# Second mixture: its first eight tiles from what two of four groups of rows fill, with the table of tiles made in two halves

## What is computed

```python
ln1_out = _layernorm(hidden_states, ln1_weight, ln1_bias)
...                                   # attention over pairs, projection
hidden_after_attn = hidden_states + proj_out
ln2_out = _layernorm(hidden_after_attn, ln2_weight, ln2_bias)
x = ln2_out.reshape(-1, H)            # H = 256
gate = jax.nn.softmax(jnp.einsum('th,eh->te', x, router_weight), axis=-1)
top_probs, top_idx = jax.lax.top_k(gate, TOP_K)           # TOP_K = 2 of 8 experts
h_mid = jax.nn.gelu(jnp.einsum('th,ehf->etf', x, moe_w1)) # 256 -> 512
expert_out = jnp.einsum('etf,efh->eth', h_mid, moe_w2)    # 512 -> 256
weights = jnp.sum(jnp.where(top_idx[None] == e_ids, top_probs[None], 0.0), axis=-1)
moe_out = jnp.einsum('eth,et->th', expert_out, weights).reshape(S, B, H)
return hidden_after_attn + moe_out
```

## Time and profile before

| | |
|---|---|
| median of 3 runs | 1021.64 us (1018.97 to 1023.74) |
| profiled execution | 1022.95 us, span of its instructions 1021.2 us |
| TensorE busy with products | 906.8 us (89%) |
| VectorE busy | 801.2 us (78%) |
| ScalarE busy | 731.2 us (72%) |
| POOL busy | 605.9 us (59%) |
| mean granted clock of TensorE | 0.938 |

### The profile page before, as it was taken

The page is one execution under the profiler, slowest core; times in us unless marked ns, Lnnn a source line. Parts: engine busy times, 40 slices in busy tenths (PEclk is TensorE's granted clock), DMA queues, the critical chain, the costliest instruction groups (busy, mean ns, idle before and its releaser), DMA issues. The chain is left out here.

```text
span 1021.2 us, 22434 instructions
## 1 busy us (share of the span) xinstructions
PE 906.8 (89%) x6180; PEld 805.9 (79%) x6180; DVE 801.2 (78%) x2324; ACT 731.2 (72%) x1651; POOL 605.9 (59%) x699
## 2 busy tenths in 40 slices
PE   7899999999999999999999848879966751799997
PEld 5579989999999999998989736669945551599996
DVE  7589999999999999999989798757657786244443
ACT  2378889899899999999989747326654741566663
POOL 2298878877777676765555354660265278145444
PEclk8999999999999999999999968999978875799999
DMA  9276666777666666676666140347762624254453
GB/s 309 55 204 192 191 181 189 194 198 201 184 196 189 191 190 189 191 213 168 212 178 194 46 154 16 117 151 227 240 207 63 238 91 153 75 81 74 76 84 48
DMA packets 111427, 162.14 MB, mean 159 GB/s; under 512 B 16201, under 2 KB 85193, under 8 KB 110282
## 3 DMA queue, kind: packets, MB, share of 16 engines
q1 hardware_dynamic: 100200, 140.56, 46.3%
q0 software_dynamic: 10224, 18.00, 8.3%
q10 hardware_dynamic: 882, 2.14, 0.7%
HBM read 110.31 MB, written 25.17 MB: 133 GB/s over the span
## 5 line engine op out<-in xcount | busy, mean ns | idle before, releaser
L2380 POOL TENSOR_SCALAR probs<-probs,inv_sum 128x1024 f32<-128x1024 f32 (+3 forms) x128 | 303.2, 2368 | 6.7 <-DVE inv_sum L2547 6.7
L2526 DVE TENSOR_TENSOR pT_lo<-t_ps,pT_hi 128x512 fp32r<-128x512 f32 (+1 forms) x320 | 198.3, 634 | 9.1 <-ACT pT_hi L2410 7.0
L2438 ACT ACTIVATE probs<-probs,neg_max 128x1025 f32<-128x1025 f32 (+7 forms) x256 | 196.8, 771 | 5.3 <-DVE neg_max L2501 5.3
L2410 ACT ACTIVATE pT_hi<-t_ps 128x512 fp32r<-128x512 f32 (+1 forms) x320 | 172.7, 551 | 31.5 <-PE t_ps L2617 18.0
L2501 DVE CUSTOM_DVE_ANT_0 probs<-s_ps,bias_set,neg_null 128x512 f32<-128x512 f32 (+3 forms) x256 | 160.6, 645 | 2.2 <-PE s_ps L2582 2.0
L2617 PE MATMUL t_ps<-ident,probs 128*128 128x128 f32 x1152 | 157.6, 273 | 0.2 <-POOL probs L2380 0.2
L2617 PEld LDWEIGHTS t_ps<-ident,probs 128*128 128x128 f32 x1152 | 136.8, 141 | 24.1 <-issue 2.3
L2632 PE MATMUL o_ps<-pT_hi,values 128*128 128x256 f32 x576 | 148.4, 287 | 1.0 <-DVE pT_lo L2526 1.0
L2581 PE MATMUL s_ps<-k_hi,q_hilo 128*128 128x512 f32 (+3 forms) x384 | 144.7, 380 | 4.1 <-DVE q_lo L2517 1.5
L2633 PE MATMUL o_ps<-pT_lo,values 128*128 128x256 f32 x576 | 145.6, 281 | 0.0
L2582 PE MATMUL s_ps<-k_lo,q_one 128*128 128x512 f32 (+3 forms) x384 | 133.7, 348 | 0.0
(11 more groups left out here) (385 smaller groups left out, 2155.8 us busy)
## 6 DMA issues: line engine op xcount, KB each, us to landing
bias_set<-bias_dram SPq DMA_DIRECT2D x16, 1024.0 KB, 5.4
bias_set<-bias_dram SPq DMA_DIRECT2D x16, 896.0 KB, 5.3
bias_set<-bias_dram SPq DMA_DIRECT2D x16, 768.0 KB, 4.9
bias_set<-bias_dram SPq DMA_DIRECT2D x16, 640.0 KB, 4.5
q_hilo<-q_hi SPq DMA_DIRECT2D x128, 64.0 KB, 2.0
q_hilo<-q_lo SPq DMA_DIRECT2D x128, 64.0 KB, 2.0
q_one<-q_hi SPq DMA_DIRECT2D x128, 64.0 KB, 2.1
bias_set<-bias_dram SPq DMA_DIRECT2D x16, 512.0 KB, 5.5
```

The source lines that it names most:

```text
L2380: pool.tensor_scalar(keys, keys, inv_sum[:, x.set, 0, h:h + 1], None, ALU.mult).then_inc(normed, 1)
L2410: act.activation(pT_hi[n % 3][:, 0:count, :], t_ps[n % 3][:, 0:2 * P * count], ACT.Copy).then_inc(hi_out, 1)
L2438: act.activation(p, p, ACT.Exp, scale=-1.0, bias=neg_max[:, x.set, row.unit, h:h + 1], accum_out=row_sum[:, x.set, row.unit, h:h + 1]).the ...
L2526: dve.tensor_tensor(pT_lo[n % 3][:, 0:count, :], t_ps[n % 3][:, 0:2 * P * count].rearrange("p (n q) -> p n q", n=count), pT_hi[n % 3][:, 0 ...
```

## The change

Four things change.

The table is made by a new class, `SplitTable`. `first_half` runs on VectorE after `sum_up(1)`, from the slabs as groups 0 and 1 left them: it counts only full tiles (`full_tiles`), of which there are at least nine, and makes the first eight entries. The rest (`second_half`) is cut into four parts, which run on VectorE inside the second mixture, ahead of its first tiles' outputs; it places what is left of each expert behind the full tiles. The experts are therefore gone through twice: the sequence of tiles is now expert 1 (4 tiles), 2 (5), 5 (3), and then 1 (6), 2 (5), 3, 4 (3), 5 (5), 6, 7 (3), 36 in all.

SP loads the first eight tiles after the scatters of groups 0 and 1 (`early_scattered`) and the stores of groups 0 to 2 (`first_stored`), and stores group 3 and writes the padding behind these loads. The wait for padding, late scatters and the rest of the table moves ahead of tile 8.

On VectorE `weights_low(4)` moves from ahead of the gates of group 2 to behind `sum_up(3)`, `sum_up(2)` moves ahead of `place(2)`, and `make_table` between `place(3)` and the last three `weights_low` goes away.

On TensorE, POOL and VectorE the mixture's waits for words are cut in two in the same way. The wait for all weights stands behind the turning of the first two tiles.

```diff
+class SplitTable:
+    FULL = EARLY_GROUPS * GROUP * TOP
...
+    def first_half(self, dve, room, ready, words_ready, clear_ready):
+        these = slice(0, self.FULL)
+        now = slice(0, BUFS)
+        self.tiles(dve, rt.full_tiles, EARLY_GROUPS, -(P - 1) / (2.0 * P))
+        self.firsts(dve, rt.full_first, rt.full_tiles)
...
+        begun, over, tile_row = self.place(dve, room, these, rt.full_first, rt.full_end, rt.full_row)
...
+        dve.tensor_copy(rt.row_of[:, now], rt.rows_f[:, now]).then_inc(ready, 1)
...
+    def second_half(self, dve, part, ready, words_ready, clear_ready):
+        rest = slice(BUFS, ROUTED)
+        if part == 0:
+            self.tiles(dve, rt.n_tiles, GROUPS, (P - 1) / (2.0 * P))
+            self.settle(dve, dve.tensor_tensor(rt.n_tiles[:], rt.n_tiles[:], rt.full_tiles[:], ALU.subtract))
+            self.firsts(dve, rt.first_tile, rt.n_tiles)
...
@@ pair_attention_stage, sync @@
+            for g in range(GROUPS - 1):
+                store(g, first_stored)
+            sp.wait_ge(table_ready, 1)
+            at = first_rows(nc, rt, len(first))
+            sp.wait_ge(first_stored, 16 * (GROUPS - 1) * B)
+            sp.wait_ge(early_scattered, 16 * EARLY_GROUPS * GROUP * TOP)
+            for k in range(len(first)):
+                sp.dma_start(first[k], routed_rows[bass.ds(at[k], P), :]).then_inc(first_in[k], 16)
+            store(GROUPS - 1, last_stored)
             sp.wait_ge(slabs_ready, 1)
             store_padding(sp, nc, rt, routed_rows, padded)
-            sp.wait_ge(table_ready, 1)
-            at = first_rows(nc, rt, len(first))
-            sp.wait_ge(stored, 16 * (1 + GROUPS * B))
-            sp.wait_ge(padded, 16 * E)
-            sp.wait_ge(scattered, 16 * NT * TOP)
-            for k in range(len(first)):
-                sp.dma_start(first[k], routed_rows[bass.ds(at[k], P), :]).then_inc(first_in[k], 16)
@@ pair_attention_stage, vector @@
             sum_up(1)
+            table.first_half(dve, table_room, table_ready, words_ready, clear_ready)
             shifts(1, 3)
-            weights_low(4)
             gates(2)
             choose(2)
             top_weights(2)
+            sum_up(2)
             place(2)
-            sum_up(2)
             sum_up(3)
+            weights_low(4)
             gates(3)
             choose(3)
             top_weights(3)
             place(3)
-            make_table(dve, rt, table_step, table_ready, slabs_ready, words_ready)
+            table.slabs(dve, slabs_ready)
             weights_low(5)
             weights_low(6)
             weights_low(7)
@@ second_mixture_stage @@
         def _(sp):
+            sp.wait_ge(table_ready, 2)
+            sp.wait_ge(padded, 16 * E)
+            sp.wait_ge(scattered, 16 * (GROUPS - EARLY_GROUPS) * GROUP * TOP)
...
             for i in range(ROUTED):
                 low(i + 3)
                 hidden_low(i + 1)
+                if i < 3:
+                    table.second_half(dve, i + 1, table_ready, words_ready, clear_ready)
...
             turn_rows(0)
             turn_rows(1)
+            pe.wait_ge(words_ready, 1)
+            words = expert_words(nc, rt, mybir.EngineType.PE, 0, 1)
+            pe.wait_ge(w_lo_ready, E)
             up(0)
```

More of the change, by code:

```diff
@@ L1056, in pair_attention_stage @@
 def pair_attention_stage(nc, block, sbuf, psum, sem, aps, keep, routing, routed_rows, parts, out):
-    xs, yacc, ident, power4, w2, w2_hi, w_in, w_used, scattered, smalls, loaded, first, first_in, w_proj, done_sems, first_pair, words_ready, w_lo_ready, out_stored = keep
+    xs, yacc, ident, power4, w2, w2_hi, w_in, w_used, scattered, smalls, loaded, first, first_in, w_proj, done_sems, first_pair, words_ready, w_lo_ready, out_stored, table, early_scattered, second_sems = keep
     ln1_w, ln1_b, ln2_w, ln2_b, w_qkv, w_router = smalls
@@ L1088, in pair_attention_stage @@
         table_room = lT[1][0:1].rearrange("o c n -> o (c n)")
-        rt.begun, rt.over, rt.tile_row = (table_room[:, ROUTED * E * i:ROUTED * E * (i + 1)].rearrange("o (n e) -> o n e", e=E)
-                                          for i in range(3))
         gate = sbuf(st, "pa_gate", [P, GROUP, E])
@@ L1144, in _, with store @@
             sp.dma_start(out[T:OUT_ROWS, :].rearrange("(n p) d -> p n d", p=P),
-                         rt.padding[:, 0:D].unsqueeze(1).broadcast_to([P, 1 + SPARES, D])).then_inc(stored, 16)
+                         rt.padding[:, 0:D].unsqueeze(1).broadcast_to([P, 1 + SPARES, D])).then_inc(last_stored, 16)
             tiles = out[0:T, :].rearrange("(n p) d -> p n d", p=P)
-            for g in range(GROUPS):
+            def store(g, stored):
                 sp.wait_ge(summed, g + 1)
@@ L1937, in second_mixture_stage @@
 def second_mixture_stage(nc, block, sbuf, psum, sem, keep, ln, routing, routed_rows, target):
-    ident, w_hi, w_lo, rows, rows_in, y, words_ready, w_lo_ready = keep
+    ident, w_hi, w_lo, rows, rows_in, y, words_ready, w_lo_ready, scattered, table, second_sems = keep
     ln_w, ln_b, w_qkv = ln
@@ L2045, in hidden_low @@
                 dve.tensor_tensor(h_lo[i % 2][:], h_ps[i % 2][:], h_hi[i % 2][:].bitcast(F32), ALU.subtract).then_inc(h_lo_ready, 1)
-            dve.wait_ge(words_ready, 2)
-            of = experts(nc, rt, mybir.EngineType.DVE)
             low(0)
             low(1)
+            dve.wait_ge(words_ready, 1)
+            words = expert_words(nc, rt, mybir.EngineType.DVE, 0, 1)
+            table.second_half(dve, 0, table_ready, words_ready, clear_ready)
             low(2)
@@ L2081, in up @@
                     cols = slice(F2 * c, F2 * c + F2)
-                    high, low = (w[:, bass.ds(of(i), 1), cols] for w in (w_hi, w_lo))
+                    high, low = (w[:, bass.ds(expert_in(words, i), 1), cols] for w in (w_hi, w_lo))
                     pe.matmul(u_ps[i % 2][:], x_hi[i % 2][:, c, :], high, start=(c == 0), stop=False)
@@ L2115, in _ @@
                 turn_rows(i + 3)
+                if i + 2 == BUFS:
+                    pe.wait_ge(words_ready, 2)
+                    words = words + expert_words(nc, rt, mybir.EngineType.PE, 1, WORDS)
                 up(i + 2)
@@ L3092, in program @@
                     w2_hi = sbuf(second, "w2_hi", [P, E, W2COLS], F32R)
+                    rt.place_split(sbuf, second)
                     rows = [flat(xs)[:, ROW * i:ROW * i + ROW] for i in range(BUFS)]
@@ L3096, in program @@
                                                                    (ln1_w, ln1_b, ln2_w, ln2_b, w_qkv, w_router), loaded,
-                                         rows, rows_in, inputs.w_raw, done, first_pair, second_words, w2_lo_ready, out_stored), rt, routed_rows, parts, out)
+                                         rows, rows_in, inputs.w_raw, done, first_pair, second_words, w2_lo_ready, out_stored, table, early_scattered,
+                                         second_sems), rt, routed_rows, parts, out)
                     middle.close()
                     second_mixture_stage(nc, block, sbuf, psum, sem, (ident[:], w2_hi, w2, rows, rows_in, [yacc[:, i, :] for i in range(BUFS)],
-                                                                 second_words, w2_lo_ready),
+                                                                 second_words, w2_lo_ready, second_scattered, table, second_sems),
                                          (ln2_w, ln2_b, w_qkv), rt, routed_rows, out)
```

160 lines of the change are left out of this document (100 added, 60 removed).

## The result

The changed kernel takes 1004.14 us in the median of four runs (1002.52 to 1004.81), the kernel before 1022.69 beside it (four runs, 1018.97 to 1026.75). The ratio is 0.9828, with a 95% interval of 0.9802 to 0.9853: by the ratio 17.6 us less, by the two medians 18.6. The prediction was 1008.6, with a range of 1003.5 to 1017.

What follows compares the result with a forecast made beforehand. TensorE's 24.5 us hole, closed by a chain over POOL's scatters and SP's loads, was taken as the bound. 18.0 − 3.9 − 1.1 = 13.0 us gained, so median 1021.64 becomes 1008.6, range 1003.5 to 1017.

Steps and rivals of the forecast that it cites:

- The likeliest case: Whole kernel: TensorE's hole closes 18.0 us earlier, then late rows cost part of it; 1008.6 us, chance 0.62.
- the places of the rows: Second mixture: tile i+8 loads into tile i's place only after its accumulation, limiting the gain to 9.5 to 16.5 us.
- The 858.9: TensorE's first up-product: predicted start in us, low weights done at 858.2 plus 0.43 for the first low half, against 876.93.
- First half of the table: VectorE, from the sum of group 1: 25 instructions taking 4.3 us unpaused; could be 10 with pauses.
- pauses in the table: VectorE's first half: 5.0 us of old pauses recur, or SP stalls at two lists; gain 5 to 9.5 us, chance 0.20.
- SP's queue: SP, third store to tile 8: stalled entries at 0.75 us each put the end some 20 us late; chance 0.04.
- Placing of group 2, 0.65 us late: VectorE: a sum ahead of the placing starts it at about 842.3, not 841.65, delaying POOL's late scatters.
- first accumulation at 876.5: POOL: late scatters end at 873.1, then reading words takes at most 3.1 us; the old start was 887.55.
- So it waits 3.9 us in all over tiles 8 to 10: TensorE: tile 10's rows arrive at 892.4 but are wanted at 888.6, leaving 14.1 of the 18.0 us.
- My bound on the gain, 890.6 less the first accumulation: Whole kernel: gain is 890.6 minus POOL's first accumulation start, 9.5 to 16.5 us for starts between 881 and 874.
- Second half of the table and later words, 1.1 us: Second mixture: table pieces on VectorE and word reading on TensorE's queue cost 1.1 us; bounds 0 and 5.
- POOL is not held: POOL: weight instructions do not hold its scatters, so tile 10's rows come in time; 1004.5 us, chance 0.08.

Runs made afterwards that it cites:

- late_rows: The changed kernel, but SP loads the first eight tiles at the old place, behind the fourth store, padding and all scatters: 1023.63 us, ratio 0.9976.
- pool_delay6: The changed kernel with 20 chained memsets on POOL between its last scatter and the first accumulation: 1017.58 us, ratio 0.9933.
- scatter_late: The changed kernel with POOL held for 12 chained memsets ahead of its last four scatters: 1003.93 us in its one run.
- order_alone: The kernel before with only VectorE's new order, table and SP unchanged: 1025.03 us, ratio 0.9993.
- warm: The changed kernel with 16 useless products on TensorE behind the turning of the first two tiles' rows: 1014.6 us, ratio 0.9907.

## Why the prediction was right, and where it was wrong

*The likeliest case named the right mechanism for the gain, and a wrong bound on it.* The time, 1004.1 us, lies 4.5 below the forecast and close to the lower end of the range, which held it because it reached up to the full 18 us. That bound, the places of the rows, did not act. The hole closes because eight tiles' rows come early (late_rows). It was to close 18.0 us earlier; the first up-product came 19.8 us earlier, 18.6 without the 1.27 us of the stretch ahead. (The 858.9 is 858.2 and 0.7 us, not 0.43; 0.68 were measured from the weights' end to the up-product.)

*First half of the table:* 4.3 us, without pauses. Measured 832.06 to 836.02, 3.96. The 5 us of pauses of the old table did not move along, nor did SP's: its eight row numbers were read and the loads went out at 844.82, and the rows were turned at 848.21, 9 us before TensorE could use them. The rivals of pauses in the table and of SP's queue fall for this kernel.

*Placing of group 2, 0.65 us late:* it was 0.2 us early (840.19 + 1.27 against 841.65). The sum put ahead of it fills the 0.87 us in which VectorE had waited for the counts there, and the gates began 0.3 us earlier instead of 0.24 later.

*The step that failed is POOL's: "first accumulation at 876.5".* It started at 870.31. Of the 6.2 us between, 1.3 are the stretch ahead and 0.8 the placing. The row of scatters, with one of 7.15 us in its midst as predicted, took 1.4 less than thought: the moved weights added 0.9 us to one scatter and the small operations 0.3 in all, where I had 1.1 and 1, and the rest was counted 0.5 too long (the hold was put at 6.3 us, though 6.97 less 0.96 is 6.0; it was 6.2). And 2.7 us are the words for POOL's waits. I had them read behind the last scatter for 3.4 us; POOL's queue reads them while the scatters run, and 0.69 us is left. pool_delay6 took that cover away, and there stood 3.56 us.

*"So it waits 3.9 us in all over tiles 8 to 10":* it waits 0. The formula itself held. The third accumulation stands at 879.60, 9.3 us behind the first, where it was 9.6; with 4.3 to SP's load and 2.1 for it, tile 10's rows are there at 886.0, and TensorE turns them at 887.83. Some 1.8 us were spare. (In the trace the load goes out at 884.08, so that 1.6 are left.) By that spare scatter_late's 2.6 us should have cost 0.8; they cost 2.9, of which 2.08 are the words on TensorE's queue, a cost of being late that the prediction did not have. My bound on the gain, 890.6 less the first accumulation, gives 19.0 us at 871.6 (870.31 and the 1.27 of the stretch ahead), more than the hole had to give. The ceiling of 18 applied, not the bound.

*Second half of the table and later words, 1.1 us:* 30.73 less 29.66, 1.07. The sum agrees by luck, for it is made of other parts. By the turning of tile 4, 0.4 us are lost because TensorE's first products run longer at the lower clock (granted 0.50 from 857.1 to 861.6, where it was at 0.99 from 880.2, 3.3 us behind the first up-product). Some 0.2 are lost at tile 4's up-product, whose low half stands behind a piece of the table on VectorE, and 0.6 at the words, which I had at 1.

*The sum* was 18.0 − 3.9 − 1.1 = 13.0. It measured 18.6 − 0 − 1.1, with some 0.5 more by the end, where the last 114 us ran at a mean granted clock of 0.99 against 0.98: 18.0 in the stage, 19.3 in the span.

*The rivals.* The time is that of "POOL is not held" (1004.5, chance 0.08), but POOL is held, for 7.15 us: until 0.8 us after the two low halves (856.35 and 0.74) that follow the weights without a gap. This disagrees once more with what the Trainium skill infers ("SBUF — State Buffer", section "Who interferes with whom"). I had tied "no wait at tile 10" to "no hold", though a shorter reading of the words does the same. Pauses came after all, in another place: not in the table, where I gave them 0.20, but on ScalarE in the mixture, and only in some sets of runs. There they cost about 6 us and would have made the time 1010.8, near the forecast for a wrong reason.

*What stays open* is the pause. It is shown that it needs no alteration of the kernel, that it is not decided by ScalarE's place in its own stream, that TensorE stands still beside it in some profiles, and that in two sets all profiles of kernels with early rows have it and in three none. Single runs of 1010 to 1012 us in the other sets may be the same thing; they were not profiled. In the six profiles that have it, ScalarE went on with the fifth tile's features 2.3 to 2.8 us after the start of POOL's last scatter, so it may end with the scatters' transfers. That was only read off; the run meant to test it had no pause. In late_rows and order_alone, on chip A, ScalarE came to these instructions 15 us or more after the last scatter and met none. The Trainium skill ("Runtime: NRT & Kernel Launch", section "Instruction fetch mechanics") has instructions fetched by DMA in blocks, and mostly hidden. This case's traces list such transfers, and one speaks against a block that came late: in warm, where ScalarE stands from 867.5 to 874.3 us, none starts between 866.8 and 879.6. What it waits for is not shown.

## What to carry to other kernels

Price a wait by what its queue can do ahead of it: reading registers beside queued work cost 0.69 us on POOL and 0.31 on TensorE here, and 3.56 and 2.08 when something stopped the queue. So a short wait can cost more than its length, and the name in a bracket must be checked against what the code waits for. When a bound of the form "gain at most X less the start of Y" decides the forecast, work out the spare on either side of it, since an error of 2 us in Y turns a cost of 4 us into none. And measure an unaltered kernel in each set of runs: without it, the 6 us that came with the chip would have been put down to the edits.

## What was not expected of the hardware

The same program took 1004.1 us in two sets of runs and 1010.8 in a third, with five runs there within 2.5 us, while the kernel before it differed by no more than 2.1 us between these sets (1022.69, 1022.24 and 1024.35). The untouched stretch ahead of the change moved too: the sum of group 1 started at 830.92, 833.88 and 830.63 us in three profiles of the same kernel. And pauses of 5.2 us in all on another engine went with a stage 5.9 us longer when TensorE's clock fell with them, and with 3.5 when it did not: with the clock at 0.52 in the window behind, the products of one tile's up-product started 0.43 us apart instead of 0.23.
